# Queries kept in SBUF and split by GpSimd, and softmax sums finished for two chunks at a time

## What is computed

```python
h = _ln(x, g1, be1)
q = (h @ Wq1).reshape(b, n, 16, 64)          # k and v likewise, from h
sim = jnp.einsum('bihd,bjhd->bhij', q, k) * 64 ** (-0.5)
attn = jax.nn.softmax(sim, axis=-1)
out = jnp.einsum('bhij,bjhd->bihd', attn, v).reshape(b, n, 1024)
x = out @ Wo1 + bo1 + x
```

## Time and profile before

| | |
|---|---|
| median of 3 runs | 1985.43 us (1984.62 to 1986.59) |
| profiled execution | 1986.85 us, its span 1985.1 us |
| granted PE clock | 1.00 of full over the whole span |
| PE busy | 1971.6 us, 99% of the span |
| DVE, ACT, POOL busy | 1393.6, 1150.6, 1444.1 us |
| self-attention chunks (S of chunk 0 to S of chunk 63) | 60.8 to 1446.5 us |
| an ordinary chunk | 19.50 us |
| chunk with a v slot, chunk with output products | 30.65 us, 30.8 to 31.0 us |

### The profile page before, as it was taken

The page is one execution under the profiler, slowest core; times in us unless marked ns, Lnnn a source line. Parts: engine busy times, 40 slices in busy tenths (PEclk is TensorE's granted clock), DMA queues, the critical chain, the costliest instruction groups (busy, mean ns, idle before and its releaser), DMA issues.

```text
span 1985.1 us, 32079 instructions
## 1 busy us (share of the span) xinstructions
PE 1971.6 (99%) x12056; PEld 1345.1 (68%) x12056; DVE 1393.6 (70%) x2382; ACT 1150.6 (58%) x2042; POOL 1444.1 (73%) x752
## 2 busy tenths in 40 slices
PE   9999999999999999999999999999999999999999
PEld 7555655667565556755655666565569999888888
DVE  6688687666768786587687666767867888744443
ACT  6665576565556665465666555656756766533332
POOL 3699899978979997899799798979896665200000
PEclk9999999999999999999999999999999999999999
DMA  7301000011000000020000001010030420000100
GB/s 256 138 38 64 17 22 22 12 33 54 22 12 12 33 12 33 1 75 11 11 12 22 33 12 54 22 33 1 22 106 22 150 65 1 1 22 33 33 11 32
DMA packets 40506, 77.63 MB, mean 39 GB/s; under 512 B 5920, under 2 KB 29600, under 8 KB 38304
## 3 DMA queue, kind: packets, MB, share of 16 engines
q1 hardware_dynamic: 40352, 75.59, 11.5%
HBM read 51.46 MB, written 24.12 MB: 38 GB/s over the span
## 4 chain that ended last, share of the span: by engine, by line
PE 92%; DVE 3%; POOL 3%; issue 1%; ACT 1%; POOLq 0%; DVEq 0%
PE score L577 21%; PE score L556 18%; PE score L703 9%; PE attn_project L512 8%; PE attn_project L688 5%; PE attn_project L717 5%; PE score L524 5%; PE score L658 4%; PE score L626 3%; PE attn_project L538 3%; PE first_score L538 3%; PE score L562 3%; POOL acc L1528 2%; PE first_score L672 1%; PE first_score L588 1%
## 5 line engine op out<-in xcount | busy, mean ns | idle before, releaser
L1528 POOL TENSOR_TENSOR acc<-acc,pT 128x1024 f32<-128x1024 f32 x384 | 916.7, 2387 | 54.4 <-POOL acc L1528 0.9
L1271 ACT ACTIVATE pT<-score 128x1024 f32<-128x1024 f32 x512 | 515.7, 1026 | 89.1 <-PE score L562 53.5
L556 PE MATMUL score<-qk 64*128 64x512 f32 x3072 | 467.5, 405 | 2.5 <-DVE hT L852 1.9
L577 PE MATMUL score<-pT,vT 128*64 128x512 f32 x1952 | 432.3, 595 | 0.0
L556 PEld LDWEIGHTS score<-qk 64*128 64x128 f32 x3072 | 267.2, 184 | 97.0 <-ACT pT L1271 20.9
L907 DVE TENSOR_REDUCE nmax<-first_score 128x2 f32<-128x1024 f32 x256 | 311.0, 1215 | 2.4 <-PE first_score L538 2.4
L907 DVE TENSOR_REDUCE nmax<-attn_project 128x2 f32<-128x1024 f32 x256 | 311.0, 1215 | 1.0 <-PE attn_project L538 0.9
L577 PEld LDWEIGHTS score<-pT,vT 128*64 128x64 f32 x1952 | 134.7, 137 | 259.5 <-issue 252.6
L1525 POOL TENSOR_TENSOR acc<-pT 128x1024 f32<-128x1024 f32 x64 | 153.4, 2396 | 68.6 <-ACT pT L1271 68.6
L512 PE MATMUL attn_project<-hT,wqk 128*128 128x512 f32 x738 | 186.3, 401 | 0.0
L703 PE MATMUL score<-hT,wp 128*128 128x512 f32 x768 | 183.7, 395 | 0.0
(11 more groups left out here) (201 smaller groups left out, 3007.2 us busy)
## 6 DMA issues: line engine op xcount, KB each, us to landing
wqk<-wqk_parts SPq DMA_DIRECT2D x24, 512.0 KB, 3.3
xres<-x_middle SPq DMA_DIRECT2D x10, 512.0 KB, 3.7
raw_v<-in_L_xattn_Wv SPq DMA_DIRECT2D x8, 512.0 KB, 4.9
keys_all<-keys SPq DMA_DIRECT2D x1, 4096.0 KB, 13.1
values_all<-values SPq DMA_DIRECT2D x1, 4096.0 KB, 13.2
wqk_parts<-wqk SPq DMA_DIRECT2D x8, 512.0 KB, 3.3
out_x<-xres SPq DMA_DIRECT2D x7, 512.0 KB, 3.0
xres<-in_x SPq DMA_DIRECT2D x3, 1024.0 KB, 5.7
```

The lines of the kernel that those rows point to most:

```text
L556: last = e.matmul(bank, key_part(P, h, r, jt), queries1[P % 2][r, w, c * BANK:(c + 1) * BANK], start=(fresh and part == 0), stop=(not fres ...
L577: last = e.matmul(banks[bank][head * DH:(head + 1) * DH, :], vT[:, v_slot(D, jt), c0:c0 + DH], pT[:, jt, head, :], start=(jt == 0), stop=( ...
L1271: e.activation(pT[:, jt].rearrange("p h n -> p (h n)"), SC[R % 2][:, :], ACT.Exp).then_inc(s.exponential, 1)
L1528: e.tensor_tensor(total, total, pT[:, jt], ALU.add).then_inc(s.probs_added, 1)
```

## The change

- **Queries.** Except for the first three query units (`FIRST_QUERIES`), ACT no longer rounds the queries out of PSUM: it copies them, scaled and unrounded, to SBUF (`queries_whole`, which lies in the place of the lo part). One chunk later ACT rounds them there to hi (`round_queries`, between the shift copies L1280 and `write_oT` L1294 of before), and POOL subtracts hi from them in place (`split_queries`, after the last add of that chunk). DVE's L897 is gone in 61 slots, and bank PJ is free after ACT's copy.
- **Sums.** `folded` has room for two chunks, and the sum of chunks C - 2 and C - 1 is taken in even slots only: one quadrant matmul with 64 columns, two reciprocals of 64 x 32 and one spread over 1024 columns. Odd slots have none.
- `maxima` is stored in 36 instead of 64 columns and `rsum` in the place of `folded`, for room. No instruction is added or moved by this.

```diff
             through = ("S1b", "S0b", "S1a")
-            if 1 <= C < NC - 1:
-                jobs += [("sum", C - 1, "T1")]
+            if C and c == 0:
+                jobs += [("sum", range(C - CHUNKS, C), "T1")]
...
+        def queries_unit(C):
+
+            P, c = divmod(C, CHUNKS)
+            return [(P + 1 + c, 3 - c)] if C >= 0 and P + 1 + c < B * PAIRS else []
...
@@ PE
-                free[bank] = ((s.split_lo, qk_of[P, u]),)
+                free[bank] = ((s.split_lo, keys_of[P, u]) if u < 2 else queries_rest((P, u)) if (P, u) in FIRST_QUERIES
+                              else (s.queries_kept, queries_of[P, u] - len(FIRST_QUERIES)),)
...
-                e.matmul(banks[bank][:, 0:2 * QB], quads[:, :], folded[:, :], start=True, stop=True
-                         ).then_inc(s.summed, 1)
+                e.matmul(banks[bank][:, 0:n * 2 * QB], quads[:, :], folded[:, first:first + n, :].rearrange("p c n -> p (c n)"),
+                         start=True, stop=True).then_inc(s.summed, 1)
@@ DVE
-                    if job[0] == "qk":
-                        split_qk(*job[1:])
+                    if job[0] == "qk" and job[2] < 2:
+                        change_keys(*job[1:])
@@ ACT
-                    e.activation(queries1[P % 2][:, 0, (u - 2) * BANK:(u - 1) * BANK], banks[bank], ACT.Copy, scale=SCALE
-                                 ).then_inc(s.split_hi, 1)
+                        e.activation(queries_whole[P % 2][:, span], banks[bank], ACT.Copy, scale=SCALE
+                                     ).then_inc(s.queries_kept, 1)
...
+            def round_queries(P, u):
+                span = slice((u - 2) * BANK, (u - 1) * BANK)
+                need.wait_ge(s.queries_kept, queries_of[P, u] - len(FIRST_QUERIES))
+                e.copy(queries1[P % 2][:, 0, span], queries_whole[P % 2][:, span]).then_inc(s.queries_hi, 1)
...
                     make_shift(C + 1)
+                for unit in queries_unit(C - 1):
+                    round_queries(*unit)
                 write_oT(C)
@@ POOL
+            def split_queries(P, u):
+                span = slice((u - 2) * BANK, (u - 1) * BANK)
+                need.wait_ge(s.queries_hi, queries_of[P, u])
+                e.tensor_tensor(queries1[P % 2][:, 1, span], queries_whole[P % 2][:, span],
+                                queries1[P % 2][:, 0, span].bitcast(F32), ALU.subtract).then_inc(s.queries_lo, 1)
...
                     if C == NC - 1 and jt in (2, 4):
                         scale_oT(C - 3 + jt // 2)
+                for unit in queries_unit(C - 1):
+                    split_queries(*unit)
```

More of the change, by code:

```diff
@@ L117, in block_kernel @@
         SQUARE = 32
-        maxima = sb("maxima", [PART, 2, SQUARE])
+        maxima = sb("maxima", [PART, SQUARE + TPC])
         keys_full = sb("keys_full", [PART, BANK // 2])
@@ L140, in block_kernel @@
             ("wo1", [PAIRS, DIM], F32R))
+        _, qk1_whole, _, qk0_whole = overlay(
+            ("before_qk", [PRING * N + 3 * TILES * BANK + (2 * ARING + 1) * BANK], F32), ("qk1_whole", [4 * N + BANK], F32),
+            ("sums_between", [2 * BANK], F32), ("qk0_whole", [4 * N + BANK], F32))
         PAIR = BANK // 2
+        queries_whole = [tile[:, N:2 * N] for tile in (qk0_whole, qk1_whole)]
         queries1 = [tile[:, 0:2 * N].rearrange("p (w n) -> p w n", w=2) for tile in (qk0, qk1)]
@@ L287, in block_kernel, with queries_rest @@
         keys_of = numbered((P, u) for P in range(B * PAIRS) for u in range(CHUNKS))
+        queries_of = numbered((P, u) for P in range(B * PAIRS) for u in range(2, 2 + CHUNKS))
+        FIRST_QUERIES = [(0, 2), (0, 3), (1, 2)]
+        def queries_rest(unit):
+            if unit in FIRST_QUERIES:
+                return s.first_queries_lo, queries_of[unit]
+            return s.queries_lo, queries_of[unit] - len(FIRST_QUERIES)
         def rows_there(key):
@@ L549, in score @@
                 if part < len(TERMS):
-                    for u in (2 + c, jt // TPC):
-                        need.wait_ge(s.split_hi, qk_of[P, u])
-                        need.wait_ge(s.split_lo, qk_of[P, u])
+                    need.wait_ge(s.queries_hi, queries_of[P, 2 + c])
+                    need.wait_ge(*queries_rest((P, 2 + c)))
+                    need.wait_ge(s.split_hi, keys_of[P, jt // TPC])
+                    need.wait_ge(s.split_lo, keys_of[P, jt // TPC])
                     if part == 0:
@@ L581, in attend, with sum_quads @@
                     free[bank] = ((s.oT_written, C + 1),)
-            def sum_quads(C, bank):
-                need.wait_ge(s.acc_folded, C + 1)
+            def sum_quads(chunks, bank):
+                first, n = chunks[0] % CHUNKS, len(chunks)
+                need.wait_ge(s.acc_folded, chunks[-1] + 1)
                 need.wait_ge(s.quads_made, 4)
                 bank_free(bank)
-                e.matmul(banks[bank][:, 0:2 * QB], quads[:, :], folded[:, :], start=True, stop=True
-                         ).then_inc(s.summed, 1)
-                free[bank] = ((s.sum_inverted, C + 1),)
+                e.matmul(banks[bank][:, 0:n * 2 * QB], quads[:, :], folded[:, first:first + n, :].rearrange("p c n -> p (c n)"),
+                         start=True, stop=True).then_inc(s.summed, 1)
+                free[bank] = ((s.sum_inverted, sum_of(chunks[0])),)
             def out1_whole(b, t, bank):
@@ L923, in turn_max @@
                         last = e.transpose(maxima_T[head * DH:head * DH + SQUARE, q:q + SQUARE],
[L924 removed]
+                                           maxima[q:q + SQUARE, head * TPC:head * TPC + SQUARE])
                 last.then_inc(s.max_turned, 1)
@@ L929, in fold_sums, with invert_sums @@
                 need.wait_ge(s.probs_added, (TILES - 1) * (C + 1))
[L930 to L931 removed]
+                need.wait_ge(s.sum_inverse, sum_of(C - CHUNKS) if C >= CHUNKS else 0)
+                e.tensor_reduce(folded[:, C % CHUNKS], acc[:, C % ARING].rearrange("p h (b n) -> p (h b) n", n=SQUARE), AX.X, ALU.add,
                                 apply_transpose=True).then_inc(s.acc_folded, 1)
[L934 to L936 removed]
+            def invert_sums(chunks, bank):
+                first, n = chunks[0] % CHUNKS, len(chunks)
+                need.wait_ge(s.summed, sum_of(chunks[0]))
                 for head in range(2):
                     r = slice(head * DH, (head + 1) * DH)
[L939 removed]
+                    last = e.reciprocal(rsum[r, first:first + n, :], banks[bank][r, 0:n * 2 * QB].rearrange(
+                        "p (c h q) -> p c h q", h=2, q=QB)[:, :, head, :])
                 last.then_inc(s.sum_inverted, 1)
[L941 to L944 removed]
+                need.wait_ge(s.sum_inverted, sum_of(chunks[0]))
+                need.wait_ge(s.oT_scaled, max(chunks[-1] - 1, 0))
+                e.transpose(sums[:, first:first + n, :].rearrange("p c (b n) -> p (c b) n", n=SQUARE),
+                            rsum[:, first:first + n, :].rearrange("p c q -> p (c q)").unsqueeze(2).to_broadcast(
+                                [PART, n * QB, SQUARE])).then_inc(s.sum_inverse, 1)
             def split_wo1(q):
@@ L1245, in split_qk @@
                 if u >= 2:
-                    e.activation(queries1[P % 2][:, 0, (u - 2) * BANK:(u - 1) * BANK], banks[bank], ACT.Copy, scale=SCALE
-                                 ).then_inc(s.split_hi, 1)
+                    span = slice((u - 2) * BANK, (u - 1) * BANK)
+                    if (P, u) in FIRST_QUERIES:
+                        e.activation(queries1[P % 2][:, 0, span], banks[bank], ACT.Copy, scale=SCALE
+                                     ).then_inc(s.queries_hi, 1)
+                    else:
+                        e.activation(queries_whole[P % 2][:, span], banks[bank], ACT.Copy, scale=SCALE
+                                     ).then_inc(s.queries_kept, 1)
                     return
```

49 lines of the change are left out of this document (21 added, 28 removed).

## The result

| | before | after |
|---|---|---|
| median | 1986.01 us (4 runs, 1984.62 to 1988.19) | 1997.09 us (4 runs, 1996.51 to 1997.83) |
| ratio of the times | | 1.0055, 95% interval 1.0038 to 1.0072 |
| profiled execution, span | 1986.85, 1985.1 us | 1997.83, 1995.9 us |
| granted PE clock, mean | 1.000 | 0.997 |

The forecast was 1983.5 us, the range 1974 to 1993. The kernel got 11 us slower instead of 2 us faster. Of the executions behind the experiments two took nearly twice as long (3860.1 and 3859.8 us); the ratios leave them out.

The account below looks back on a forecast made before the run. PE leads the chunks, POOL has least room and leads the end. PE's -14.5 us plus waits of 3.8, 4.2 and 1.5 give -5.0; the end's +3.1 makes -1.9: 1983.5 us, range 1974 to 1993.

Parts of the forecast that it names:

- Exponentials 6 and 7 have the attend stage as cover.: In each chunk, only exponential 5, needed by score block 7, hurts when late; POOL may be 11.7 us late.
- the forecast's own limit: POOL's scaling may start 11.7 us after a chunk's first score; each further us holds PE one us.
- PE waits 3.8 + 4.2 + 1.5 us.: PE's waits on late POOL: 3.8 us in chunks 1 to 7, 4.2 in 8 to 15, 1.5 in five later groups.
- Slot 13's late copy and turns: Slot 13, with its layer norm: late last exponential delays ACT's copy and the turns; 2.7 us of PE's waits.
- The gain of PE, -14.5 us.: To the start of chunk 56, before POOL's waits: L897 removed and fewer sums, less costs, save PE 14.5 us.
- the spread: Slots 12, 28 and 44: the double spread delays DVE's L847, for which PE waits; 0.53 us each, 1.6 in all.
- The sums' part: Before chunk 56: dropped quadrant sums save 6.7 us; wider sums cost 0.5 and the double spread 1.6.
- The split at 1.25 us.: POOL's 128 x 512 query split costs 1.25 us between queued instructions, like its scaling; bounds 1.20 and 1.35.
- The end is led by POOL, +3.1.: From chunk 56, POOL's count decides: six splits, less waits used up, add 3.1 us; PE's gains do not matter.
- Rival 2: In chunks, POOL's lateness bites earlier, through ACT's queue; limit 9.07 gives +12.7 us, 10.2 gives +5.6; 22%.
- Rival 1: In chunks, POOL holds PE up far less; sum -5.3 us, or -12.1 if no chunk waits; 20%.
- rival 3: Chunks gain nothing, scores still take 9.27 us; 9.9 us of gain go, POOL's waits return 5; 1988.1 us; 13%.

Follow-up runs that it names:

- the bank experiment: Whole change, but in 17 late chunks attend writes to bank T0 instead of S0a; 1993.89 us, ratio 1.004 to the kernel before.
- The best version: Whole change with query rests on DVE from SBUF, early units split from PSUM, fold moved, late spread, 8 spare columns; 1974.99 us, 0.9943 of the kernel before.
- the sums alone: Kernel before plus only the two-chunk sums; queries rounded and split from PSUM as before; 1988.26 us, ratio 1.001.
- the rests on DVE: Whole change, but DVE instead of POOL subtracts hi from the queries in SBUF, behind its fold; 1981.42 us, ratio 0.9973 to the kernel before.

## Why the prediction was wrong, step by step

In span, the forecast was -1.9 us and the trace has +10.8. Of the 12.7 us between them 11.8 lie between the starts of chunk 0 and chunk 56 (forecast -5.0, measured +6.8): 5.5 are waits on POOL, 3.2 the clock behind them, 3.1 a smaller gain of PE. From chunk 56 on the forecast was +3.1 and the trace has +4.1.

- *"Exponentials 6 and 7 have the attend stage as cover."* This is the step that failed. Exponential 7 has that cover; exponential 6 has not, since attend's first matmul writes the bank that it reads. The limit is 10.4 us, shown by the table of chunks, and by the bank experiment, in which the forecast's own limit came back. The code for it, `products_bank` returning S0a, was there to be read. An estimate of its worth: if the waits of each of the seven groups of chunks fall by 1.3 us, or to nothing where they are shorter, 7 of the 15.0 us are left, so the step accounts for some 8 us of waits. No run shows this sum, since the other bank has a price of its own.
- *PE waits 3.8 + 4.2 + 1.5 us.* Measured: 5.9 in chunks 5 to 7, 2.6 in chunk 15, 6.5 in the five later groups; and 3.2 us by a lower clock behind the waits of chunks 7 and 15, for which the forecast had no term. Slot 13's late copy and turns, 2.7 us of its sum, did not happen, which hid part of the miss.
- *The gain of PE, -14.5 us.* Too large by some 3 us: chunk 56 came 6.8 us late with 15.0 us of waits and 3.2 of clock, which leaves a gain of 11.4. The best version, whose chunks hardly wait, gained 11.2 us up to there. Attend moved by 0.18 us only in odd chunks; in even ones it moved by 0.12 (9.27 to 9.15). Behind slots 12, 28 and 44 the spread cost 0.73 us each (first exponential at S + 2.92 instead of 2.19), not 0.53. The sums' part was well sized, 4.1 us against 4.6.
- *The split at 1.25 us.* Right, between queued instructions; its records mean 1290 ns. The rule of the Trainium skill, GPSIMD Engine Reference, Elementwise — side-by-side cycle accounting (twice VectorE's time) would have it at 1.35 to 1.38, an estimate from L897's 0.69 us; the trace has 1.9 times that in the record and 1.8 from start to start.
- *The end is led by POOL, +3.1.* The size, 4.1, is near it by luck. Chunk 63 gave 4.6 us away inside its scores, where PE waited for the fold of chunk 62 and then ran at a lower clock, and the fold behind the chunk waited 0.82 us for POOL, not 6. The sum ahead of block 6 was not followed.
- *`maxima` and `rsum` move no instruction.* True, and still they cost 1.6 us in the last stages: they move every tile behind them.
- *Rivals.* Rival 2 named the right direction and, at 10.2 us, a limit near the measured one, but by another mechanism (ACT's queue behind the last exponential); its +5.6 us lacked the clock, chunk 63 and the tiles. Rival 1 is excluded by POOL, which waits only 7.1 us for exponentials in all chunks (68.6 before), rival 3 by attend at S + 9.09.

## What to carry to other kernels

When work goes to the engine with the least room, find the limit of its lateness by listing, for each buffer and bank that its late result holds, who writes it next: the first reader of the result may have cover where the next writer of the bank has none. A stage that occurs once (here the last chunk, with other work ahead of the fold) can eat what dozens of regular ones gain (4.3 us against 4.1 with the sums alone), so its timeline is read too. Give the late engine the work only in the stages where a trace shows it ahead, and after any change of tile sizes look at matmul distances in stages that were not touched.

## What the runs showed of the hardware

- PE idled 2.5 of 4 us (from 208) and 3.2 of 4 us (from 1458), and stretches of 0.65 and 0.50 granted clock followed (212 to 216, 1462 to 1466), so that a wait of 2.6 us cost 4.1 in chunk 7. In chunk 5 it idled 2.4 of 4 us and the clock stayed at 1.00.
- DVE and POOL operations that both read two SBUF operands hold each other up: DVE's 128x512 ends 0.55 us behind the POOL instruction that runs when it starts (58 of 65 in the trace with the rests on DVE), so it lasts 0.65 to 2.9 us, and POOL's next 128x1024 add lasts 2.66 us instead of 2.40.
- A shift of the operands by 32 bytes of a partition changed the distance of the feed-forward's 512-column matmuls from 232.6 to 234.0 ns, one by 32 bytes the other way to 233.3.
- The stream transpose of 128x1024 takes 1.25 us, of 128x512 0.71. A slot with a quadrant sum of 64 columns is 0.23 us longer than one without (10.25 against 10.02 from attend to the next S); with 32 columns it was 10.23.
